# A four-layer graph kernel on one Trainium2 core: the front state's node form made by VectorE blocks and transfers, the opening and the first pair pass written as one order, biases loaded as rows

## The reference

```
h = x                                             # layer 0: three gated steps
for _ in range(3):
    a  = adj @ h ;  av = [a, a]
    z  = sigmoid(av W3' + w3_b + h U3' + u3_b)
    r  = sigmoid(av W4' + w4_b + h U3' + u3_b)
    hv = tanh(av W5' + w5_b + (r*h) U5' + u5_b)
    h  = (1 - z) * h + z * hv
x = norm(x + h)
rel = adj.T * (q k') ; rel = rel / |rel|_row      # layer 1: masked attention, q, k, v = x Wq', x Wk', x Wv'
x = norm(x + rel v)
x = norm(x + (adj @ x) W + b)                     # layer 2
x = norm(x + norm_adj @ (x W) + b)                # layer 3, norm_adj = D^-1/2 adj D^-1/2
```

## Time and profile before

| | before |
|---|---|
| device time, three runs | 1271.56, 1271.95, 1273.86 us (median 1271.95) |
| the profiled execution's own time | 1271.8 us |
| its span, first to last instruction | 1270.0 us |
| granted TensorE clock, mean | 0.995 |
| busy: TensorE, VectorE, ScalarE, GpSimd | 98%, 81%, 46%, 15% |
| TensorE instructions | 7664 matmuls, transposes among them |

### The profile page before, as it was taken

The page is one execution under the profiler, slowest core; times in us unless marked ns, Lnnn a source line. Parts: engine busy times, 40 slices in busy tenths (PEclk is TensorE's granted clock), DMA queues, the critical chain, the costliest instruction groups (busy, mean ns, idle before and its releaser), DMA issues.

```text
span 1270.0 us, 21112 instructions
## 1 busy us (share of the span) xinstructions
PE 1240.6 (98%) x7664; PEld 1103.3 (87%) x7664; DVE 1031.4 (81%) x2274; ACT 583.7 (46%) x1007; POOL 192.4 (15%) x366
## 2 busy tenths in 40 slices
PE   7799999999999999999999999999999999999996
PEld 6589899898988989899898988989889898998895
DVE  5668889788888878888788888878888788895898
ACT  4444444444444444454444444444454445444442
POOL 0001112020210202112020110202112021110023
PEclk9999999999999999999999999999999999999999
DMA  7020110202001020010202002020010202000000
GB/s 199 1 50 1 38 30 1 66 0 59 7 17 50 0 66 0 33 33 0 66 0 50 17 17 50 0 66 0 21 45 0 66 0 49 17 17 18 1 1 34
DMA packets 86168, 37.56 MB, mean 30 GB/s; under 512 B 64768, under 2 KB 83200, under 8 KB 86144
## 3 DMA queue, kind: packets, MB, share of 16 engines
q1 hardware_dynamic: 84592, 36.71, 10.6%
q0 software_dynamic: 192, 0.52, 0.2%
q10 hardware_dynamic: 1360, 0.01, 0.1%
HBM read 20.45 MB, written 8.39 MB: 23 GB/s over the span
## 4 chain that ended last, share of the span: by engine, by line
PE 94%; DVE 4%; DMA 1%; POOL 1%; issue 0%; ACT 0%; ACTq 0%; DVEq 0%
PE b_ps L430 46%; PE f_ps L430 43%; PE f_ps L525 2%; PE b_ps L525 1%; DMA bias_in<-in_L_gnn_u_b 1%; PE b_ps L571 1%; DVE f_stats L1251 0%; DVE hf_feat L1267 0%; DVE normed L1267 0%; POOL f_rstd L364 0%; DVE f_cand L1184 0%; DVE b_stats L1251 0%; DVE f_kept L1178 0%; ACTq L827 0%; DVE f_a_lo L1162 0%
## 5 line engine op out<-in xcount | busy, mean ns | idle before, releaser
L362 POOL TENSOR_TENSOR b_var_eps<-b_moments,eps 128x2 f32<-128x2 f32 x120 | 44.1, 368 | 827.6 <-DVE b_moments L1258 827.6
L364 POOL TENSOR_TENSOR b_rstd<-b_var_eps,neg_half 128x2 f32<-128x2 f32 x120 | 97.0, 808 | 9.4
L866 ACT ACTIVATE f_z<-f_ps,bias_z 128x512 f32<-128x512 f32 x66 | 45.2, 685 | 92.5 <-PE f_ps L430 92.5
L870 ACT ACTIVATE f_cand<-f_ps,bias_c 128x512 f32<-128x512 f32 x66 | 45.5, 690 | 85.1 <-PE f_ps L430 85.1
L1168 DVE TENSOR_TENSOR f_gate<-f_gate,hf_feat 128x512 f32<-128x512 f32 x66 | 45.2, 685 | 46.2 <-ACT f_gate L858 46.0
L1251 DVE BATCH_NORM_STATS2 b_stats<-b_ps 128x6 f32<-128x256 f32 x180 | 68.3, 421 | 13.9 <-PE b_ps L430 13.3
L430 PE MATMUL f_ps<-adjT_hi,hf_node_hi 128*128 128x256 f32 x264 | 74.6, 283 | 0.0
L430 PE MATMUL f_ps<-adjT_hi,hf_node_lo 128*128 128x256 f32 x264 | 74.3, 282 | 0.0
L430 PE MATMUL f_ps<-adjT_lo,hf_node_hi 128*128 128x256 f32 x264 | 74.2, 281 | 0.0
L1290 DVE TENSOR_TENSOR b_rh_lo<-b_ps,b_rh_hi 128x512 fp32r<-128x512 f32 x90 | 61.9, 688 | 13.7 <-ACT b_rh_hi L824 13.4
L824 ACT ACTIVATE f_a_hi<-f_ps 128x512 fp32r<-128x512 f32 x66 | 39.0, 593 | 71.8 <-PE f_ps L430 71.8
(11 more groups left out here) (325 smaller groups left out, 4610.5 us busy)
## 6 DMA issues: line engine op xcount, KB each, us to landing
x_front<-in_x SPq DMA_DIRECT2D x16, 512.0 KB, 3.5
x_blocks<-in_x SPq DMA_DIRECT2D x60, 128.0 KB, 3.4
input_t<-hf_feat SPq DMA_DIRECT2D x15, 512.0 KB, 2.9
out<-result SPq DMA_DIRECT2D x15, 512.0 KB, 3.0
b_cand<-in_L_gnn_u_w SPq DMA_DIRECT2D x2, 256.0 KB, 8.9
bias_out<-in_L_gnn_bias POOLq DMA_DIRECT2D x4, 128.0 KB, 6.3
b_z<-in_L_gnn_w_w SPq DMA_DIRECT2D x1, 512.0 KB, 11.4
b_gate<-in_L_gnn_w_w SPq DMA_DIRECT2D x1, 512.0 KB, 12.4
```

Source lines behind the costliest of these rows:

```text
L364: pool.tensor_tensor(Y.rstd[:, g], Y.var_eps[:, g], neg_half[:], ALU.pow).then_inc(Y.s_rstd, 1)
L866: act.activation(L.z[:, k], L.ps0[:, k], ACT.Sigmoid, bias=bias_z[:, k:k + 1]).then_inc(L.s_z, 1)
L870: act.activation(L.cand[:, k], L.ps1[:, k], ACT.Tanh, bias=bias_c[:, k:k + 1]).then_inc(L.s_tanh, 1)
```

## The change

Five things change; what is computed stays.

1. For pairs 1 to 14 the state after the first step is no longer turned by TensorE. `turn_state` transposes 32 x 32 blocks on VectorE into the tile front.gate, `move_blocks` brings the blocks to their partitions by 16 transfers of 32 KB from SBUF to SBUF (front.gate to front.z) on SyncE's queue, and ScalarE (`moved_hi`) and VectorE (`moved_lo`) split from there. `turn_h(state_f, ...)` stays for pair 0 and in `finish`.
2. The opening and `body(1, 0)` become one written order `start()` on every engine; each matrix is waited for where it is first used.
3. The gate biases are loaded as rows (two rows of 512 bytes each) into a [10, 128] tile, turned by one TensorE transpose into front.ps1, copied and added by VectorE. It is TensorE's first instruction.
4. The broadcast of the layer biases waits for the load of w5.
5. The orders in `body` and `finish` are written anew, with the same instructions otherwise; the degree and centring work of VectorE is cut into pieces and placed apart.

```diff
+            def move_blocks(S, turn):
+                sp.wait_ge(S.s_blocks, 2 * turn)
+                for a in range(4):
+                    for b in range(4):
+                        sp.dma_start(S.moved[32 * a:32 * a + 32, b],
+                                     S.blocks[32 * b:32 * b + 32, a]).then_inc(S.s_moved, 16)
...
                 keep_input(p)
+                move_blocks(state_f, p)
                 store(main, p - 1)
...
+            pool.wait_ge(s_load["w5"], 16)
             for i, b in enumerate((l2_b, l3_b)):
...
+            def turn_biases():
+                pe.wait_ge(s_consts, 5)
+                pe.wait_ge(s_load["bias"], 16 * 5)
+                pe.transpose(bias_turned, bias_rows[:], ident[0:5 * C, 0:5 * C]).then_inc(s_bias_turned, 1)
...
@@ body, TensorE
-                update(back, q, 0)
+                for k in range(2):
+                    update(back, q, k)
+                mix(front, 2 * p, 0, p)
                 candidate_mixed(back, q, 1)
                 candidate_mixed(back, q, 0)
-                candidate_reset(back, q, 0)
-                update(back, q, 1)
-                for k in range(2):
-                    mix(front, 2 * p, k, p)
-                candidate_reset(back, q, 1)
-                for k in range(2):
-                    base(front, 2 * p, k, p)
+                mix(front, 2 * p, 1, p)
+                for k in range(2):
+                    candidate_reset(back, q, k)
+                base(front, 2 * p, 0, p)
                 reset(front, 2 * p, 0)
+                base(front, 2 * p, 1, p)
                 turn_sum(main, q, 0)
                 reset(front, 2 * p, 1)
+                update(front, 2 * p, 0)
                 turn_sum(main, q, 1)
-                update(front, 2 * p, 0)
+                update(front, 2 * p, 1)
                 candidate_mixed(front, 2 * p, 0)
-                keys(main, q, 0)
-                update(front, 2 * p, 1)
                 candidate_reset(front, 2 * p, 0)
-                relate(main, q, 0)
-                keys(main, q, 1)
                 candidate_mixed(front, 2 * p, 1)
                 candidate_reset(front, 2 * p, 1)
+                for k in range(2):
+                    keys(main, q, k)
                 values(main, q, 0)
+                relate(main, q, 0)
+                values(main, q, 1)
                 relate(main, q, 1)
-                for k in range(2):
-                    turn_h(state_f, 2 * p + 1, k)
-                values(main, q, 1)
+                base(front, 2 * p + 1, 0)
                 sum_squares(main, q, 0)
                 attend(main, q, 0)
-                mix(front, 2 * p + 1, 0)
+                base(front, 2 * p + 1, 1)
+                for k in range(2):
+                    mix(front, 2 * p + 1, k)
                 sum_squares(main, q, 1)
                 attend(main, q, 1)
-                mix(front, 2 * p + 1, 1)
-                for k in range(2):
-                    base(front, 2 * p + 1, k)
                 reset(front, 2 * p + 1, 0)
                 mix_nodes(main, q, 0, 0)
...
@@ start, TensorE, up to the pair pass
+                turn_biases()
+                prepare(0)
+                turn_first(0)
+                prepare(1)
+                turn_first(1)
+                for k in range(2):
+                    mix(front, 0, k)
+                prepare(2)
+                base(front, 0, 0)
+                prepare(3)
+                base(front, 0, 1)
+                reset(front, 0, 0)
+                prepare(4)
+                reset(front, 0, 1)
+                prepare(5)
+                for k in range(2):
+                    update(front, 0, k)
+                candidate_mixed(front, 0, 0)
+                candidate_reset(front, 0, 0)
+                candidate_mixed(front, 0, 1)
+                candidate_reset(front, 0, 1)
+                prepare(6)
+                query_key_matrix()
+                for k in range(2):
+                    turn_h(state_f, 1, k)
+                base(front, 1, 0)
+                for k in range(2):
+                    mix(front, 1, k)
+                base(front, 1, 1)
+                for k in range(2):
+                    reset(front, 1, k)
+                candidate_mixed(front, 1, 1)
+                update(front, 1, 0)
+                candidate_mixed(front, 1, 0)
+                candidate_reset(front, 1, 0)
+                update(front, 1, 1)
+                candidate_reset(front, 1, 1)
+                prepare(8)
+                for k in range(2):
+                    turn_h(state_b, 0, k)
+                mix(front, 2, 0, 1)
+                mix(back, 0, 0)
+                mix(front, 2, 1, 1)
+                mix(back, 0, 1)
...
@@ ScalarE
-                act.dma_start(bias_in[:, i, :], b.rearrange("(c p) -> p c", p=P),
-                              allow_slow_non_contiguous=True).then_inc(s_load["bias"], 16)
+                act.dma_start(bias_rows[C * i:C * i + C], b.rearrange("(c p) -> c p", p=P)).then_inc(s_load["bias"], 16)
...
+            def moved_hi(S, v, g, turn):
+                act.wait_ge(S.s_moved, 256 * turn)
...
+                rows = S.moved[:, :, g * P:(g + 1) * P].rearrange("p q (u i) -> p u q i", i=32)
+                copy(S.node_hi[:, g].rearrange("p h (c q i) -> p (h c) q i", q=4, i=32), rows).then_inc(S.s_node_hi, 1)
...
@@ body, ScalarE, around the wait for the transfers
+                values_hi(main, q, 1)
                 relation_hi(main, q, 1)
+                for k in range(2):
+                    moved_hi(state_f, 2 * p + 1, k, p)
                 relation_squares(main, q, 1)
...
@@ VectorE
+            def turn_state(S, v, c):
+                dve.wait_ge(S.s_feat, upto(v, c))
+                out = S.blocks.rearrange("p q (u c i) -> p u q c i", c=C, i=32)[:, :, :, c]
+                dve.transpose(out, S.feat[:, c].rearrange("p (u q i) -> p u q i", q=4, i=32)).then_inc(S.s_blocks, 1)
+
+            def moved_lo(S, v, g):
+                dve.wait_ge(S.s_node_hi, upto(v, g))
...
+                dve.tensor_tensor(cells(S.node_lo), rows, full(cells(S.node_hi)), ALU.subtract).then_inc(S.s_node_lo, 1)
...
@@ body, VectorE, around the turn and around moved_lo
+                candidate_part(front, 2 * p, 0)
+                first_h(p, 0)
+                turn_state(state_f, 2 * p + 1, 0)
+                candidate_part(front, 2 * p, 1)
+                first_h(p, 1)
+                turn_state(state_f, 2 * p + 1, 1)
                 keys_lo(main, q, 0)
...
                 relation_lo(main, q, 1)
+                for k in range(2):
+                    moved_lo(state_f, 2 * p + 1, k)
                 sum_attended(main, q, 0)
```

More of the change, by code:

```diff
@@ L480, in mix @@
                     pe.wait_ge(state_b.s_node_lo, upto(pair - 1, k))
+                if not later(n):
+                    pe.wait_ge(s_prep_lo, 8 if L is back else 1)
+                if L is front and not later(n):
+                    pe.wait_ge(s_bias, 5)
                 for g in range(G):
@@ L502, in reset @@
                 pe.wait_ge(L.s_a_lo, upto(n))
+                if L is front and not later(n):
+                    pe.wait_ge(s_prep_lo, 3)
                 product(L.ps0[:, k], columns(w4T, k), mixed(L), start=False).then_inc(L.s_reset, 1)
@@ L507, in update @@
                 pe.wait_ge(L.s_r, upto(n, k))
+                if L is front and not later(n):
+                    pe.wait_ge(s_prep_lo, 4)
                 product(L.ps0[:, k], columns(w34T, k), mixed(L), start=False).then_inc(L.s_update, 1)
@@ L512, in candidate_mixed @@
                 pe.wait_ge(L.s_a_lo, upto(n))
+                if L is front and not later(n):
+                    pe.wait_ge(s_prep_lo, 5)
                 product(L.ps1[:, k], columns(w5T, k), mixed(L), stop=False)
@@ L785, in _ @@
-            pe.wait_ge(s_prep_lo, 5)
-            for k in range(C):
-                update(front, 0, k)
-            for k in range(C):
-                candidate_mixed(front, 0, k)
-            pe.wait_ge(s_prep_lo, 6)
-            for k in range(C):
-                candidate_reset(front, 0, k)
-            pe.wait_ge(s_centred, 3)
-            turn_matrix(6, wv_nat)
-            query_key_matrix()
-            for g in range(G):
-                turn_h(state_f, 1, g)
-            for k in range(C):
-                base(front, 1, k)
@@ L800, in _ @@
-            for k in range(C):
-                mix(front, 1, k)
-            pe.wait_ge(s_rows, 1)
-            turn_matrix(8, adj_rows)
-            for k in range(C):
-                reset(front, 1, k)
-            for k in range(C):
-                update(front, 1, k)
-            for k in range(C):
-                candidate_mixed(front, 1, k)
-            for k in range(C):
-                candidate_reset(front, 1, k)
-            for g in range(G):
-                turn_h(state_b, 0, g)
@@ L1343, in body @@
+                rh_lo(back, q, 0)
+                reset_h(back, q, 1)
```

(44 more changed lines are left out.)

1096 lines of the change are left out of this document (700 added, 396 removed).

## The result

The changed kernel is slower: a median of 1336.68 us (four executions, 1316.92 to 1338.54) against 1272.86 us for the kernel before beside it. The ratio is 1.042, with a 95% interval of 1.029 to 1.056; the medians alone are 1.050 apart, because the comparison leaves out the two slowest executions, which lie over 1.5% above the fastest. The time goes with the clock: 1316.92 us at a mean granted clock of 0.987, 1336.6 at 0.965. The profiled execution took 1338.54 us, with a span of 1336.5 us, 66.5 more than before.

The account below looks back on a forecast made before the run. TensorE, busy 98% of the span, was taken as the bound, with holes in the opening. 1271.8 - 6.6 (turn) - 9.6 (opening) = 1255.6 us, order and end at 0; forecast 1252 to 1261, range 1246 to 1274.

Parts of the forecast that it names:

- rival B: ScalarE's wait for the 16th transfer: issues at 0.59 us make it slower, 1287 us; chance 0.14 with its near side.
- Part 1: Front state's turn leaves TensorE in pairs 1 to 14: 12.2 us off, 0.4 us stall a pair, net gain 6.6 us.
- the spacing of the issues: Sixteen transfers on the sync queue, taken 0.44 us apart (ends 0 and 0.59), last landing at 11.55 us.
- the price of a wait: TensorE at mix(front): expected stall 0.4 us in each pair, subtracted one for one from the turn's 0.87 us.
- The queue behind the wait: ScalarE and VectorE work behind the transfers, needed at reset(front, 2p+1, 0): costed at 0, range 0 to 0.4 us per pair.
- 0.5 us of slack at the reset: At reset(front, 2p+1, 0): 1.9 us before a_lo(1) is needed, a_hi and a_lo need 1.35, so 0.5 spare.
- Part 2: New order of the pair pass: taken at 0, bounds -0.1 and +0.5 us per pair.
- Part 3: Biases and opening: first mix of the pair pass at 53.75 instead of 63.35 us, gain 9.6, bounds 3 and 12.
- the cold stretch: The opening's stretch ahead of the first pair pass where the granted clock falls; claimed to stay.
- the walk of wk: Opening: wk load taken at 19 us again, putting rh_lo(1) at 24.9, 0.3 us ahead of its use.
- Part 4: finish, the same instructions in another order: taken at 0, with 3 us either way.
- the spacing of 0.52 from which the kernel turns slower: Issue spacing on the sync queue giving a stall of 1.56 us a pair, where the opening's gain is used up.

Follow-up runs that it names:

- e6: Changed kernel with each of the sixteen transfers carrying 8 KB instead of 32, part of the node form stale; 1332.32 us in its one execution.
- e3: Changed kernel with eight of the sixteen transfers issued on SyncE's queue and eight on GpSimd's; 1259.38 us, ratio 0.990 to the kernel before.
- e5: Changed kernel with twelve transfers instead of sixteen, part of the node form stale; 1269.12 us, ratio 0.997 to the kernel before.
- e4: Changed kernel with fourteen unused 512-column matmuls filling TensorE's wait before mix(front); 1304.88 us, ratio 1.026 to the kernel before.
- e1: Changed kernel with the front state turned on TensorE again in pairs 1 to 14, no transfers; 1265.21 us, ratio 0.995 to the kernel before.
- e9: Changed kernel with its 13 loop pair passes in the old order, TensorE turning the state; 1263.04 us, ratio 0.992 to the kernel before.
- e8: As e7, with VectorE's fill(main, q, 1, 1) moved behind hand_over_h(p, 1); 1261.36 us, ratio 0.992 to the kernel before.
- e7: As e3, with the biases turned and summed later so that TensorE begins with adj; 1262.04 us, ratio 0.991 to the kernel before.
- e2: Changed kernel with one store to DRAM and four loads back in place of the sixteen transfers; 1305.47 us, ratio 1.025 to the kernel before.
- e10: Changed kernel with ten of the sixteen transfers on SyncE's queue and six on ScalarE's; 1256.86 us, ratio 0.987 to the kernel before.

## Why the prediction was wrong

The forecast was 1255.6 us, and the kernel took 1336.7. The mechanism that decided is rival B's, given a small chance and a price of 1287. The steps in turn:

- **Part 1, the spacing of the issues: this step failed.** "I take 0.44, its 0.39 and a gap of 0.05" chose the row of x_front because its runs of 1 KB look like those of the new transfers. The measured 0.634 (0.59 and a gap of 0.04) is above even the upper end of 0.59. Run length was the wrong likeness. The only SBUF to SBUF row, input_t at 0.54, was nearer, and e6 shows that size was no reason to go below it. Nearer still was a row from DRAM. The four issues of x_blocks were taken as 3.11 us together, and one by one they show, in the trace of the kernel before (duration in ns, least, median, most):

```profile
L316 SPq DMA_DIRECT2D x_blocks<-in_x x60: 582/583/4054, 14.7 to 1076.8; - x60
```

Each of them writes 32 partitions, as the new ones do, and 0.583 us against their 0.59 is the closest price of all. Whether the partitions are the reason no run shows; that x_front comes from DRAM is not, as x_blocks does too. With 0.634 the same walk gives 13.1 against 3.05 + 9.5 + 1.9 + 1.95 = 16.4, a wait of 3.3; 3.4 was measured. All its other terms (first issue, landing, copies, arrival of TensorE) were right within 0.1 us. The 2.0 us that the prediction took from the section on the anatomy of one DMA of the Trainium skill's "DMA: Bandwidth & Descriptors" are given there for transfers issued by GpSimd; the traces have 1.9 us on that queue (e3) and 1.88 on SyncE's. e3, e5 and e6 show the step in three ways.
- **Part 1, the price of a wait.** The walk charged each microsecond of waiting at one microsecond. Behind 3.3 us it cost 2.69 more, 2.41 of them because the 24 matmuls ran at the lower level of the clock (e4: 3.08 us when TensorE is kept busy). No term of the prediction had this, though the fall in the opening, a mean of 0.94, stood in the earlier trace rows, and there too TensorE had waited just before, 2.9 us until 59.88. Over fourteen passes it is 36.7 us, the larger part of what B's 1287 misses; the 0.044 us of spacing above its 0.59 are another 14 x 15 x 0.044 = 9.2.
- **The queue behind the wait.** The 0.5 us of slack at the reset held: no second wait of that kind appears in the pair. Between e1 and e3 a pair is 0.80 us shorter (76.76 against 75.96), nearly all of the turn's 0.87.
- **Part 2** was set at 0 within -0.1 and +0.5. It is +0.26 a pair (e1 against e9). The walk gave each of TensorE's operands 1 us or more; the split b_a_lo of the last convolution ahead of the turn has none and comes 0.28 us late. Which part of VectorE's new order holds it up stays open; e8 only moved it.
- **Part 3** held: first step's end 29.55 (29.4), turn of hf 31.99 (31.75), turn of hb 53.09 (51.95), first mix 55.25 (53.75); gain 8.1 instead of 9.6. Late were the first instruction, 6.41 instead of 5.5, and the first mix behind the turn of hb, 2.16 us after the turn's start instead of 1.8. One sentence was wrong, to the good: the cold stretch did not stay in this execution, the clock is 1.00 until the first long wait at mix, and the turn of hb takes 1.09 us instead of 1.97. The slip in the walk of wk (9.4 and 10.3 are 19.7, not 19) cost nothing, as wk had landed by 15. e7, the one other order tried, gave nothing back for the late biases.
- **Part 4:** -2.0, taken at 0 with 3 either way.

The chances were wrong for the same reason. The sum hung on one price, and the spacing of 0.52 from which the kernel turns slower lay below two of the three prices at hand (0.39, 0.54 and, read one by one, 0.583). I put most of the chance below it on a likeness of run length. The Trainium skill's "DMA: Bandwidth & Descriptors", section "Rules for kernel authors", spoke for coalescing transfers under 64 KB. The trace agrees that these are nearly all overhead: 10.1 us of issues for 32 KB each, and 10.08 for 8 KB each. But fewer and larger transfers were no cure by themselves (e2, 1305); spreading the same ones over two queues was (e3, e10).

## What to carry to other kernels

Count the DMA issues between a producer and its consumer, multiply by the duration of single issues in the trace, the dearest kind first (here 0.39 to 0.59 us on SyncE, and for the new transfers the same at 8 and 32 KB), and if that product is what the consumer waits for, split the issues over two queues before judging the idea. A wait of 2.3 to 4.3 us on a TensorE that is otherwise full mostly cost 1.4 to 2.7 us on top of itself here, as matmuls behind it ran at half the clock; waits of 0.7 to 1.8 us cost 0.3 on top. Where one unseen price decides the sign and the rows at hand lie on both sides of it, give neither side most of the chance.

## What the runs showed that was not expected

- The issue of an SBUF to SBUF transfer takes 0.59 us and a gap of 0.04 on SyncE and 0.50 us on GpSimd; from DRAM, x_front of 512 KB takes 0.39 to 0.40, but x_blocks of 128 KB into 32 partitions 0.58.
- SBUF to DRAM and back: 2.66 us for the store of 512 KB, then 6.55 us for the last of four loads of 128 KB.
- Waits of TensorE of 0.7 to 1.8 us kept the full clock in all passes (e5); of 2.3 to 3.1 us they lost it in nine of fourteen (e2), of 3.2 to 4.1 us in thirteen (e6), and of 3.3 to 4.3 us in all fourteen of the profiled execution of the changed kernel, for the 5.49 us of the mix in thirteen of them.
- A recorded pause of TensorE, of 0.01 us (e4, and ahead of the turn in e1) as of 0.7 us (e5), went with 0.28 us more in the piece behind it.
- With 112 transfers on GpSimd's queue the span ended 8.2 us after the last result instead of 3.3.
